# Feed-forward half of a four-block transformer layer pair: separate PSUM banks for raw products and tap sums, each convolution tap in its own slot, maxima finished through PSUM, and sixteen of sixteen chunks scaled by GpSimd

## The reference, cut to what matters

```
def act_quant(x):                       # one scale for each token
    scale = 127.0 / clip(max(abs(x), axis=-1), 1e-05)
    return clip(round(x * scale), -128, 127) / scale
def weight_quant(w):                    # -1, 0 or 1, one scale for the matrix
    scale = 1.0 / clip(mean(abs(w)), 1e-05)
    return clip(round(w * scale), -1, 1) / scale
h = act_quant(x) @ weight_quant(w1).T   # 4096 x 2048
h = depthwise_conv1d(h, conv_w, conv_b) # 3 taps along the tokens, of each channel by itself
h = silu(h)
y = act_quant(h) @ weight_quant(w2).T   # 4096 x 512
x = x + tanh(g_ffn[1]) * y
```

## Time and profile before

| | us |
|---|---|
| median of three runs | 1982.39 |
| span of the profiled execution | 1983.3 |
| the three runs | 1982.03, 1982.39, 1984.40 |
| feed-forward blocks, start of HMAX(0) of block 1 to that of block 7 | 1674.4 to 1925.5 |
| what follows to the end | 57.8 |

### The profile page before, as it was taken

The page is one execution under the profiler, slowest core; times in us unless marked ns, Lnnn a source line. Parts: engine busy times, 40 slices in busy tenths (PEclk is TensorE's granted clock), DMA queues, the critical chain, the costliest instruction groups (busy, mean ns, idle before and its releaser), DMA issues.

```text
span 1983.3 us, 24380 instructions
## 1 busy us (share of the span) xinstructions
PE 1599.7 (81%) x9442; PEld 718.8 (36%) x9510; DVE 1743.9 (88%) x2619; ACT 1485.4 (75%) x1098; POOL 616.9 (31%) x480
## 2 busy tenths in 40 slices
PE   6858966698557966785599969999999976888887
PEld 3212211122112211231244426666666632334432
DVE  6899998999999987898598877999998669999997
ACT  4899999999999999999354845554554357767771
POOL 1000000000000000000062236666666446887881
PEclk9999999999999999999799989999999988999998
DMA  5000200020000010000387753333332110432312
GB/s 199 1 0 29 79 11 1 22 75 22 1 1 1 22 54 1 1 11 1 110 312 291 265 172 100 112 112 112 107 100 81 43 37 27 79 61 70 57 43 74
DMA packets 116710, 143.66 MB, mean 72 GB/s; under 512 B 25327, under 2 KB 74607, under 8 KB 116211
## 3 DMA queue, kind: packets, MB, share of 16 engines
q1 hardware_dynamic: 116594, 142.10, 22.9%
HBM read 87.55 MB, written 50.33 MB: 70 GB/s over the span
## 4 chain that ended last, share of the span: by engine, by line
ACT 43%; PE 30%; DVE 19%; issue 4%; POOL 3%; DMA 2%; SPq 0%; DVEq 0%; another core or an unknown queue 0%; POOLq 0%; ACTq 0%
ACT unit L514 39%; PE psum L1647 5%; PE psum L1681 5%; PE psum L1633 3%; DVE hmax_parts L1429 3%; DVE psum L1418 3%; PE psum L1016 3%; PE psum L1010 3%; DVE unit L423 2%; PE psum L1657 2%; PE psum L1674 2%; POOL hidden L1837 1%; PE psum L1666 1%; PE psum L547 1%; DVE hidden_q L1453 1%
## 5 line engine op out<-in xcount | busy, mean ns | idle before, releaser
L514 ACT ACTIVATE unit<-unit 128x4096 f32<-128x4096 f32 x244 | 857.6, 3620 | 0.5 <-DVE unit L423 0.3
L423 DVE TENSOR_SCALAR unit<-feat_proj,text_proj 128x1024 f32<-128x1024 f32 x976 | 667.5, 747 | 67.2 <-PE psum L639 65.2
L639 PE MATMUL psum<-unit,w_pad 128*32 128x512 f32 x3904 | 474.8, 605 | 234.1 <-ACT unit L514 234.1
L639 PEld LDWEIGHTS psum<-unit,w_pad 128*32 128x32 f32 x3904 | 102.5, 109 | 557.3 <-ACT unit L514 398.6
L680 POOL TENSOR_SCALAR red<-red 128x8 f32<-128x8 f32 x4 | 2.0, 510 | 531.5 <-DVE red L321 531.5
L1820 POOL TENSOR_TENSOR h<-h,arow 128x512 f32<-128x512 f32 x104 | 135.7, 1318 | 73.0 <-ACT h L1582 72.8
L1699 PE MATMUL psum<-xq_block,w_q 128*128 128x512 bf16 x489 | 122.8, 391 | 27.5 <-ACT hidden L1601 21.3
L680 POOL TENSOR_SCALAR rstd<-mv 128x8 f32<-128x8 f32 (+1 forms) x5 | 1.7, 336 | 411.7 <-DVE mv L216 411.7
L547 PE MATMUL psum<-xnT,W_sb 128*128 128x512 f32 x256 | 125.2, 617 | 2.1 <-ACT xnT L465 2.1
L1589 ACT ACTIVATE psum<-h,conv_b_sb,conv_w_sb 128x512 f32<-128x512 f32 x112 | 86.2, 779 | 53.6 <-POOL h L1820 46.7
L1734 PE MATMUL psum<-w_q,hidden_q 128*128 128x512 fp8e4 x448 | 104.1, 386 | 20.8 <-ACT hidden_q L1612 12.3
(11 more groups left out here) (255 smaller groups left out, 2790.0 us busy)
## 6 DMA issues: line engine op xcount, KB each, us to landing
h_scratch<-h SPq DMA_DIRECT2D x44, 512.0 KB, 4.4
hin<-h_scratch SPq DMA_DIRECT2D x32, 704.0 KB, 4.7
xin<-in_x SPq DMA_DIRECT2D x8, 1024.0 KB, 6.7
tern_in<-in_w1T SPq DMA_DIRECT2D x16, 512.0 KB, 4.2
tern_in<-in_w2T SPq DMA_DIRECT2D x16, 512.0 KB, 6.8
x<-in_x SPq DMA_DIRECT2D x16, 512.0 KB, 3.7
x_scratch<-x SPq DMA_DIRECT2D x32, 256.0 KB, 2.0
x3in<-x_scratch SPq DMA_DIRECT2D x31, 256.0 KB, 3.1
```

The lines of the kernel that those rows point to most:

```text
L423: ins = ve.tensor_scalar(units[:, n % 3, k, :], FP[:, bi % 2, k, :], TP[:, k, n:n + 1], None, ALU.add)
L514: ac.activation(units[:, n % 3], units[:, n % 3], ACT.Tanh).then_inc(unit_tanh, 1)
L639: mm = te.matmul(psum[k * TG:(k + 1) * TG, 3 + 2 * grp + half, :], w_pad[:, k, TG - 1 - tt:2 * TG - 1 - tt], units[:, n % 3, k, half * BAN ...
```

## The change

- **Slots.** OFF2 goes from 3950 to 4120, N2 from 344 to 306, and every tuple of the feed-forward part is written anew. The chunks of a block no longer go in the order of their numbers, so waits count by position in the tuple (`nth`, `of_half`).
- **Banks.** The ring of six becomes two rings of three: raw products in the banks 0, 1, 2, tap sums in 3, 7, 5. A raw bank is free when its copy (RAW) is done; TAP0 or PTAP of a chunk waits for the SILU of the chunk three numbers before.
- **Scaling.** All sixteen chunks are copied by ScalarE and scaled by GpSimd; VMID is empty.
- **Taps.** TAPS is split in TAP1 and TAP2, each with a slot of its own.
- **Maxima.** HMAX of the second half writes into bank 6 in place of SBUF; HM2 is one scalar_tensor_tensor with that bank as an input, which also does the clip at 1e-5. S3 keeps only the reciprocal; the factor 127 goes into the copy of SROW, and the factor for OUT is made by a small ScalarE step, HS2, with `w_mean[:, 2:3]` holding the mean times the gate over 127.

```diff
+        ve.tensor_scalar(w_mean[:, 2:3], w_mean[:, 1:2], tg[:, 3:4], INV127, ALU.mult, ALU.mult).then_inc(mean_done, 1)
+        V.wait_ge(mean_done, 3)
-    N1, N2, OFF2 = 216, 344, 3950
+    N1, N2, OFF2 = 216, 306, 4120
-    GP_MID, VE_MID = (0, 1, 2, 3, 5, 6, 7, 8, 9, 10, 12, 13, 15), (4, 11, 14)
-    W1 = (98, 152, 189, 199, 208, 245, 275, 317, 327, 337, 350, 393, 403, 413, 423, 433)
-    VMID = (284, 443, 449)
-    GMID = (172, 222, 232, 242, 267, 292, 333, 344, 358, 369, 452, 463, 506)
-    TAPS = (209, 289, 302, 314, 338, 358, 371, 383, 395, 467, 479, 498, 523, 535)
+    GP_MID, VE_MID = (0, 1, 2, 3, 4, 5, 6, 7, 8, 9, 10, 11, 12, 13, 14, 15), ()
+    W1 = (34, 70, 0, 85, 150, 77, 143, 230, 194, 186, 273, 281, 237, 293, 300, 266)
+    RAW = (73, 129, 69, 135, 195, 92, 179, 263, 232, 227, 284, 293, 259, 314, 368, 280)
+    GMID = (165, 238, 123, 229, 247, 264, 282, 273, 256, 308, 317, 412, 299, 326, 403, 291)
+    TAP0 = (253, 248, 297, 308, 274, 330, 342, 357, 419, 431, 453, 476, 464, 490)
+    TAP1 = (266, 271, 304, 316, 329, 337, 349, 365, 430, 438, 461, 508, 473, 502)
+    TAP2 = (277, 294, 311, 323, 343, 354, 360, 372, 450, 444, 468, 519, 491, 513)
+    PTAP = (245, 399)
+    SILU = (288, 303, 268, 318, 336, 352, 363, 372, 425, 447, 470, 459, 482, 526, 498, 530)
-    HROUND = (798, 854, 910)
-    HMAX = (408, 579)
-    HM2 = (620,)
-    HMAXT = (656,)
-    SRED = (677,)
-    S3 = (695,)
-    HS = (724, 764, 818, 871)
-    OUT = (836, 892, 958, 1015)
+    HROUND = (728, 789, 835)
+    HM2 = (590,)
+    HMAXT = (597,)
+    SRED = (607,)
+    S3 = (618,)
+    HS2 = (748,)
+    HMAX = (384, 537)
+    HS = (642, 677, 747, 800)
+    W2 = (728, 772, 816, 963)
+    OUT = (763, 804, 903, 994)
-    RING, OUT_BANK = (0, 1, 2, 3, 7, 5), 4
+    W1_RING, TAP_RING, OUT_BANK = (0, 1, 2), (3, 7, 5), 4
+    def nth(f, c, slots, chunks):
+        at = slots[chunks.index(c)]
+        return f * len(chunks) + sum(1 for s in slots if s <= at)
+    def bank_free(engine, n):
+        if n < len(TAP_RING):
+            bank = READ_BY[TAP_RING[n]]
+            engine.wait_ge(bank_read[bank], ATT_TURNS[bank])
+        else:
+            engine.wait_ge(silu2_done, nth((n - len(TAP_RING)) // HC, (n - len(TAP_RING)) % HC, SILU, CHUNKS))
...
+            for f, c, n in of(q, TAP1, VE_TAPS):
+                acc = tap_bank(HC * f + c)
+                V.wait_ge(tap0_done, nth(f, c, TAP0, VE_TAPS))
+                scaled_by(V, f, c)
                 ve.scalar_tensor_tensor(out=acc, in0=h1[:, c, 1:BANK + 1], scalar=cw_sb[:, c, 1:2], in1=acc,
+                                        op0=ALU.mult, op1=ALU.add).then_inc(tap1_done, 1)
+            for f, c, n in of(q, TAP2, VE_TAPS):
+                acc = tap_bank(HC * f + c)
+                V.wait_ge(tap1_done, nth(f, c, TAP1, VE_TAPS))
                 ve.scalar_tensor_tensor(out=acc, in0=h1[:, c, 2:BANK + 2], scalar=cw_sb[:, c, 2:3], in1=acc,
+                                        op0=ALU.mult, op1=ALU.add).then_inc(tap2_done, 1)
...
+                ve.tensor_reduce(psum[:, 6, :] if k else hm[:, 0, :], H2[f % 2][:, pairs].rearrange("p g t r -> p t g r"),
+                                 AX.XY, ALU.max, apply_absolute_value=True).then_inc(hmax_step, 1)
-                ve.tensor_tensor(hm[:, 0, :], hm[:, 0, :], hm[:, 1, :], ALU.max).then_inc(hmax_step, 1)
+                ve.scalar_tensor_tensor(out=hm[:, 0, :], in0=hm[:, 0, :], scalar=1e-5, in1=psum[:, 6, :], op0=ALU.max,
+                                        op1=ALU.max).then_inc(bank_read[6], 1)
-                ve.tensor_scalar(hs[:, f % 2, 0, :], hs[:, f % 2, 0, :], 1e-5, INV127, ALU.max,
-                                 ALU.mult).then_inc(s_step, 1)
                 ve.reciprocal(hs[:, f % 2, 1, :], hs[:, f % 2, 0, :]).then_inc(s_step, 1)
-                ve.tensor_scalar(hs[:, f % 2, 2, :], hs[:, f % 2, 0, :], w_mean[:, 1:2], None,
-                                 ALU.mult).then_inc(s_step, 1)
...
+                ac.activation(srow[:, :], psum[:, 6, :], ACT.Copy, scale=QMAX).then_inc(bank_read[6], 1)
+            for f, k, n in before_last(at2(q, HS2)):
+                A.wait_ge(bank_read[6], turn[6]["hmaxT", f])
+                ac.activation(hs[:, f % 2, 2, :], hs[:, f % 2, 0, :], ACT.Copy,
+                              scale=w_mean[:, 2:3]).then_inc(out_scaled, 1)
...
             for f, c, n in at2(q, W1):
                 T.wait_ge(xqb_loaded, 16 * KC * (f + 1))
+                b = n - len(W1_RING)
+                if b < 0:
+                    bank = READ_BY[W1_RING[n]]
+                    T.wait_ge(bank_read[bank], ATT_TURNS[bank])
+                elif b % HC in GP_MID:
+                    T.wait_ge(raw_copied, nth(b // HC, b % HC, RAW, GP_MID))
```

More of the change, by code:

```diff
@@ L1190, in flamingo @@
     HALF = HC // 2
-    N1, N2, OFF2 = 216, 344, 3950
-    LEN1, LEN2 = 1198, 1023
+    TILES = tuple(range(TPK))
+    N1, N2, OFF2 = 216, 306, 4120
+    LEN1, LEN2 = 1198, 996
     SHIFT = (0, 156)
@@ L1291, in flamingo @@
     turn[6] = turns(first("pv", PV), first("wo", WO), second("arow", AROWMM),
-                    second("hmaxT", HMAXT), second("srow", SROWMM))
+                    ("hmax", HMAX[1:], N2, NF - 1, OFF2), second("hmaxT", HMAXT), second("srow", SROWMM))
     turn[7] = turns(first("turn2", TURN2))
@@ L1307, in upto, with of_half, scaled_by @@
         return f * len(chunks) + sum(1 for d in chunks if d <= c)
+    def nth(f, c, slots, chunks):
+        at = slots[chunks.index(c)]
+        return f * len(chunks) + sum(1 for s in slots if s <= at)
+    def of_half(f, k, slots, chunks):
+        return max(nth(f, c, slots, chunks) for c in chunks if c // HALF == k)
+    def scaled_by(engine, f, c):
+        if c in GP_MID:
+            engine.wait_ge(mid_gp, nth(f, c, GMID, GP_MID))
+        else:
+            engine.wait_ge(mid_ve, nth(f, c, VMID, VE_MID))
+    def bank_free(engine, n):
+        if n < len(TAP_RING):
+            bank = READ_BY[TAP_RING[n]]
+            engine.wait_ge(bank_read[bank], ATT_TURNS[bank])
+        else:
+            engine.wait_ge(silu2_done, nth((n - len(TAP_RING)) // HC, (n - len(TAP_RING)) % HC, SILU, CHUNKS))
     def before_last(at):
         return [(f, i, n) for f, i, n in at if f < NF - 1]
-    END_BANK, LAST_BANK = RING[0], RING[1:1 + TPK]
+    END_BANK, LAST_BANK = 0, (1, 2, 3, 7)
     def attention_over(engine):
@@ L1460, in add_rows @@
             V.wait_ge(w2_mm, TPK * f + i + 1)
-            V.wait_ge(s_step, 3 * f + 3)
+            if f < NF - 1:
+                V.wait_ge(out_scaled, ATT_EXPS + f + 1)
+            else:
+                V.wait_ge(s_step, NF + 2)
             V.wait_ge(x3in_loaded[i], TERN_LOADS + 16 * (f + 1) + (16 if i in (0, 3) else 0))
@@ L1704, in feed_forward @@
                 T.wait_ge(edges_done, edged(f, c))
-                if c in GP_MID:
-                    T.wait_ge(mid_gp, upto(f, c, GP_MID))
-                else:
-                    T.wait_ge(mid_ve, upto(f, c, VE_MID))
+                scaled_by(T, f, c)
+                bank_free(T, HC * f + c)
                 for k in range(3):
-                    mm = te.matmul(hidden_bank(HC * f + c), tapd[:, j, k, :], h1[:, c, k:k + BANK], start=(k == 0),
+                    mm = te.matmul(tap_bank(HC * f + c), tapd[:, j, k, :], h1[:, c, k:k + BANK], start=(k == 0),
                                    stop=(k == 2))
@@ L1756, in last_block @@
             mm.then_inc(spread_mm, 1)
-            T.wait_ge(hmax_step, 3 * NF + 9)
+            T.wait_ge(hmax_step, 2 * NF + 1 + 9)
             for c in range(HC):
```

126 lines of the change are left out of this document (52 added, 74 removed).

## The result

The changed kernel runs in 1966.52 us (median of 4 runs, 1966.02 to 1967.64); the kernel before, on the same chip, in 1983.17 (1982.03 to 1984.4). The ratio is 0.9918, its 95% interval [0.9905, 0.9932]: 0.8% faster, where 1948 us were forecast. The forecast's own range ended at 1955, and the one with the first two rivals at 1966. The profiled execution has a span of 1964.3 us, against 1983.3: 19.0 us less.

A forecast was written before the change was run, and what follows sets the result against it. VectorE bounds the 41.85 us period, GpSimd (38.3) after the change. Gains 21.3 (periods) + 6.6 (attention's end) + 6.3 (end) = 34.2, less 0.2: span 1949.3, median 1948 us; range 1943 to 1955, with two rivals 1935 to 1966.

The forecast's parts named there:

- the first two rivals: Four engines too near each other (1958 us, 25%); GpSimd bound, but attention's end gains 15 or exclusion partly hidden (1938, 15%).
- Six periods, -21.3: Feed-forward half, block 1's to block 7's first HMAX: each period falls from 41.85 to 38.3 us, GpSimd setting it.
- The sign that the prediction named: Steady period, if right: GpSimd busy 37 to 38 us with next to no idle time, VectorE's idle time behind it.
- HM2 with a PSUM operand, 0.66: VectorE in each period: HM2 reading one PSUM input takes 0.66 us in place of a stretched 1.6, -0.95.
- Taps apart: VectorE in each period: third taps set apart from second taps cost 0.66 instead of 0.79 us, -1.3 a period.
- TensorE's terms: TensorE in each period: W2, W1, PTAP, spreads and transposes give 35.3 us, hidden below 38.3.
- GpSimd excluded once of three: Bound for the six periods: HROUND excludes GpSimd only once of three, period 37.2 us, gain 27.9 us.
- the slower rival: Steady periods: W1 waits for raw copies in the ring of three, 0.6 us each, period 44.9, total 1988 us; 4%.
- Where attention ends, -6.6: Up to block 1's first HMAX: last tile needs 30 us, then 43 of VectorE and 5 idle; 1667.8, not 1674.4.
- The end, -6.3: Block 7's first HMAX to L1478: 25.8 us falls to 19.5, counted from VectorE's work and GpSimd's chain.
- the first (1958): Four engines too near each other, each lateness passed on: period 40 us, 1958 us; 25%.
- the third (1974): Neither gives: period at 40.5 us and attention's end at +6, 1974 us; 8%.

The follow-up runs named there:

- the kernel without the order wait: Changed kernel, but GpSimd's HS of tiles 2 and 3 no longer waits for VectorE's rounding of the tile before: 2031.76 us, ratio 1.0261.
- the first load early: Changed kernel with block 0's activation load issued at slot 3950 in place of 4144: 1957.87 us, ratio 0.9879.
- both loads early: Changed kernel with block 0's load at slot 3950 and the rows of x loaded three tiles ahead instead of two: 1954.31 us, ratio 0.9857.
- The old offset: Changed kernel with OFF2 back at 3950 instead of 4120 and block 0's load at slot 3852: 1963.96 us, ratio 0.9901.

## Why the prediction was wrong

- **Six periods, -21.3: right.** Measured -20.9 (38.37 us on the mean). The bound moved from VectorE to GpSimd. The exclusions cost GpSimd 1.16 and 1.54 us of waiting, and 1.04 of stretching (twelve GMIDs take 14.92, where the same twelve beside no rounding, in the kernel without the order wait, take 13.88): 3.7 us where 3.4 and 0.1 were forecast. The sign that the prediction named, GpSimd busy for 37 to 38 us, did not come: it is busy for 35.77, and most of the exclusion shows as idle time.
- **HM2 with a PSUM operand, 0.66: right** (0.68). That what it spares GpSimd reaches the time was assumed, and the experiment with the maxima in SBUF shows no gain in the time.
- **Taps apart: right** by mechanism, 0.12 us a pair; worth 5.8 us in all.
- **Two slips in its sums**, without effect on the forecast: TensorE's terms add to 35.5 and not 35.3, and with GpSimd excluded once of three by its own terms the period would be 36.0; 37.2 is twice of three.
- **The ring of three, the slower rival: absent in the steady periods.** TensorE waits 1.1 us in a period for raw copies. From attention's last sum to block 1's first HMAX it waits for them for 12.7 us even with the first load early; whether any of that reaches the time no run tells. The wait is real once a read of the bank stands behind a long VectorE instruction.
- **Where attention ends, -6.6: wrong, +2.7** (+4.4 counted from the mask addition). The step that failed is the sentence that one block's load "is issued in the gap in front of its first W1 of 28 us and stays hidden". The load of the first block has no such gap: the new slots put it 24 slots behind the first W1, and SyncE's queue put it behind a store that waits for VectorE. Price, by the experiment, 8.7 us. With the load early block 1's first HMAX comes within 0.1 us of the forecast position, but that is luck in two ways. The last sum comes at 1613.9 where 1619.8 was forecast, and the stretch behind it takes 53.9 us where 48 were, VectorE's 43 and 5 idle. And counted from the mask addition at 1490.90 (1489.99 and 1488.84 in the kernels with one and with both loads early), this piece gained 5.8 us of the 6.6 with this load alone early and 4.8 with both. The old offset costs 5.7 to 6.1 us.
- **The end, -6.3: wrong, -1.1.** The step that failed is the list of what comes late once the 4.70 us wait for W2 is gone. It counted VectorE and GpSimd and left out the row loads. The trace of before shows one issued in 3.98 us and landing after 12.9, behind exactly that wait. Price 3.3 us in the profile, 2.5 in the median; another 1.5 go with TensorE's clock, as I read it. With both loads early this piece is 19.94 against 19.5.
- **What is left.** The median of the kernel with both loads early is still 6 us above 1948, though its profiled execution is only 1.1 above the forecast span. Much of that nearness is luck. In every run on record that has both numbers, the time is 1.7 to 1.9 us above the span. So the profiled execution of before, with its span of 1983.3, took about 1985.1 us, above the three runs and not within their reach, and the one with both loads early (1952.16) is the fastest of its four. Of the 32.9 us between the two spans 2.1 lie ahead of the change. The rest is 4.8 where attention ends (6.6 forecast), 19.9 in the periods (21.3), 5.8 at the end (6.3) and 0.3 behind the last HMAX: 30.8 of 34.2 us in these two executions. By the medians of runs on one chip it is 28.7 us (1982.97 to 1954.31). Where the last 2 us between traces and medians lie is open, since one execution of each was profiled.
- **The rivals.** 1966.5 us lies between the first (1958) and the third (1974), and for the reason of neither: both had longer periods, and these came as forecast.

The same fault lies in both misses: SyncE's DMAs "keep their number", and I priced them at nothing without placing them. The slots and the queue were there to be read.

## What to carry to other kernels

When an order is renumbered, place each DMA again: its slot against its first consumer's, and what stands before it in its queue. When a wait is taken away, look in the trace of before for every transfer that lands during that wait, not only for the engines. And a wait that the data do not need may be what lets another engine in: before it is removed, ask who runs during it.

## What the chip showed that was not expected

- A rounding on VectorE that meets a closed row of GpSimd instructions can be held up until the row ends: 3.08 us behind GMIDs in the changed kernel, 12.14 without the order wait, 1.22 alone. If it arrives close to the boundary of two of them it gets in at once: in the kernel with the maxima in SBUF it starts at 1795.78, takes 1.22, and three GMIDs take 4.41 instead of 3.39. The rule of who wins was not measured.
- The Trainium skill's page "SBUF — State Buffer", section "Who interferes with whom", has the exclusion for a whole instruction; the traces agree, and add that it may last through several.
- Every eighth load of a tile's rows takes 3.8 to 4.0 us to issue and 12.9 to 13.1 to land, tiles 10, 18 and 26 in the kernels before and after; most others take 0.3 to 0.7 to issue. With the loads three tiles ahead the last two slow ones are those of tiles 19 and 27. Why is open.
